# Rows of the expert stages sent through DRAM, norms of 24 tiles in the setup, x in one queue, the feed-forward bias on GpSimd

## The reference

```
x = x + 0.5 * ffn(norm(x))     # 512 hidden, weights binarized, exact gelu
x = x + gated_attention(norm(x))   # groups of 32, one head, relu squared + a linear part
x = x + 0.5 * ffn(norm(x))     # same weights
x = x + 0.5 * experts(norm(x)) # below
x = x + linear_attention(norm(x))  # 16 heads of 64
x = x + 0.5 * experts(norm(x)) # same weights
```

## Time and profile before

| | us |
|---|---|
| median of 3 runs (2285.88 to 2286.19) | 2286.04 |
| profiled execution | 2280.57 |
| its span | 2278.7 |
| setup, to the first transpose of ffn0 | 23.5 |
| ffn0, to the first transpose of gau1 | 109.7 |

### The profile page before, as it was taken

The page is one execution under the profiler, slowest core; times in us unless marked ns, Lnnn a source line. Parts: engine busy times, 40 slices in busy tenths (PEclk is TensorE's granted clock), DMA queues, the critical chain, the costliest instruction groups (busy, mean ns, idle before and its releaser), DMA issues. The chain is left out here.

```text
span 2278.7 us, 42519 instructions
## 1 busy us (share of the span) xinstructions
PE 2170.7 (95%) x13706; PEld 1748.3 (77%) x13706; DVE 1522.8 (67%) x4922; ACT 1242.7 (55%) x2504; POOL 690.7 (30%) x724
## 2 busy tenths in 40 slices
PE   5989998999999999899999999999999899999995
PEld 5978888977777777777777777877777777777775
DVE  6867776876777776556565566666666666777664
ACT  4645445754554554465566665666665444545542
POOL 0412222533575655500000000000100344665545
PEclk9999999999999999999999999999999999999998
DMA  8040000000111111200000000000000011111122
GB/s 276 0 176 0 0 0 1 2 10 22 36 41 43 37 38 44 56 7 0 0 0 0 0 0 1 1 1 1 1 1 1 12 28 40 46 51 49 51 55 73
DMA packets 70648, 68.44 MB, mean 30 GB/s; under 512 B 9312, under 2 KB 57952, under 8 KB 70112
## 3 DMA queue, kind: packets, MB, share of 16 engines
q1 hardware_dynamic: 60960, 47.62, 6.6%
q0 software_dynamic: 8192, 16.79, 3.2%
q10 hardware_dynamic: 1344, 2.16, 0.4%
HBM read 32.47 MB, written 34.08 MB: 29 GB/s over the span
## 5 line engine op out<-in xcount | busy, mean ns | idle before, releaser
L2034 ACT ACTIVATE moe_fc<-moe_bank,all_b_fc 128x380 f32<-128x380 f32 (+2 forms) x448 | 245.8, 549 | 277.7 <-PE moe_bank L1964 274.6
L2141 DVE SCALAR_TENSOR_TENSOR moe_act<-moe_bank,all_b_moe_gate,moe_fc 128x380 f32<-128x380 f32 (+2 forms) x448 | 256.7, 576 | 168.3 <-PE moe_bank L1968 101.4
L1980 PEld LDWEIGHTS moe_bank<-all_w_proj,moe_act 128*128 128x128 f32 x2560 | 300.0, 192 | 12.2 <-issue 2.4
L1980 PE MATMUL moe_bank<-all_w_proj,moe_act 128*128 128x128 f32 x2560 | 305.7, 276 | 2.0 <-DVE moe_expert_out L2150 2.0
L1803 POOL DMA_INDIRECT all_landed<-rows_out,all_take_at x256 | 271.7, 1061 | 117.9 <-issue 113.4
L1494 POOL COPY lin_xn_ones<-lin_xn 128x254 f32<-128x254 f32 x32 | 12.7, 398 | 720.7 <-PE lin_bank L1244 720.4
L2041 ACT ACTIVATE moe_act<-moe_act 128x760 f32<-128x760 f32 (+2 forms) x224 | 174.7, 780 | 93.2 <-DVE moe_act L2141 92.7
L1879 POOL TENSOR_SCALAR moe_hot<-all_slot_ids,moe_slot 128x608 fp32r<-128x608 f32 x112 | 203.3, 1824 | 68.3 <-DVE moe_slot L2118 33.7
L1388 ACT ACTIVATE lin_neg<-lin_bank 128x512 f32<-128x512 f32 x256 | 151.7, 592 | 105.5 <-PE lin_bank L1236 61.9
L1286 PEld LDWEIGHTS lin_bank<-lin_kv,lin_qT 128*128 128x128 f32 x1024 | 145.0, 192 | 74.4 <-issue 62.3
L1964 PE MATMUL moe_bank<-gau_rowsT,all_w_fc 128*128 128x380 f32 (+2 forms) x448 | 170.1, 461 | 1.6 <-ACTq L2045 1.6
(11 more groups left out here) (248 smaller groups left out, 4472.8 us busy)
## 6 DMA issues: line engine op xcount, KB each, us to landing
rows_out<-moe_expert_out SPq DMA_DIRECT2D x96, 128.0 KB
rows_out<-all_zeros SPq DMA_DIRECT2D x1, 9728.0 KB, 28.7
rows_out<-moe_expert_out SPq DMA_DIRECT2D x80, 62.0 KB
all_landed<-rows_out,all_take_at POOLq DMA_INDIRECT x256, 2.7
out<-all_x SPq DMA_DIRECT2D x5, 640.0 KB, 4.5
all_w_fc<-in_w_fc SPq DMA_DIRECT2D x1, 2048.0 KB, 9.8
all_w_gate<-in_w_gate SPq DMA_DIRECT2D x1, 2048.0 KB, 13.6
all_w_proj<-in_w_proj SPq DMA_DIRECT2D x1, 2048.0 KB, 18.1
```

What stands on the lines that cost most here:

```text
L1980: last = nc.tensor.matmul(bank[OUT][:, j * DIM:(j + 1) * DIM], act_in[:, i % 2, h, j * P:(j + 1) * P], k.w_proj[:, e * MC + h, :], start=( ...
L2034: nc.scalar.activation(fc[:, j, 0:c.width], bank[FC + j % 2][:, 0:c.width], ACT.Identity, bias=k.b_fc[:, e * MC + j:e * MC + j + 1]).then_ ...
L2141: nc.vector.scalar_tensor_tensor(act_in[:, i % 2, j, 0:c.width], bank[GATE + j % 2][:, 0:c.width], k.b_moe_gate[:, e * MC + j:e * MC + j + ...
```

## The change

1. **Rows through DRAM.** Four DRAM tensors `rows_in` (`RINGS`, 609 rows of 128) take turns. After `assign`, GpSimd issues for each tile and choice an indirect DMA that scatters the 128 rows of the norm to their places (4 per batch). SyncE waits for them, and loads both halves back in blocks of 128 rows (4 DMAs per batch; 304 rows are two blocks and a third that overlaps). `send` transposes those blocks, three per half. Split, one-hots and their semaphores go; SyncE follows the slots.
2. **Slots.** Batches are routed every 4 slots instead of 5 (8 instead of 9 in the last routing chunk); load stands at lag 8, the sends at 14 and 15. Gathers and combines stay where they are. Four norms are kept instead of three.
3. **Setup.** Parts of x are 12, 12, 20 and 20 tiles, all on SyncE's queue, and the setup makes the norms of 24 tiles. ffn0 takes the statistics of part 3 in turns 0 to 4 and of part 4 in turns 8 to 12, four tiles a turn, with the norm chain's pieces in turns 4 to 7 and 12 to 15.
4. **Bias on GpSimd in ffn0**, as in ffn2; the group bias is made two buckets a turn in turns 4 to 19, spread at turn 21, and the weight difference stands at turn 28. Its inputs have a semaphore of their own, first in SyncE's queue.
5. Stage gau1 fills the four rings with zeros behind `rows_out`; GpSimd and SyncE wait for that once.

```diff
-X_PART = 16
+X_CUTS = 0, 12, 24, 44, 64
 KNOWN = 2
 LANDED = 4
+RINGS = 4
...
-                for i in range(KNOWN):
-                    sp.dma_start(k.x[:, X_PART * i:X_PART * (i + 1), :], xv[:, X_PART * i:X_PART * (i + 1), :]).then_inc(k.x_in[i], 16)
+                for i in range(4):
+                    sp.dma_start(k.x[:, X_CUTS[i]:X_CUTS[i + 1], :], xv[:, X_CUTS[i]:X_CUTS[i + 1], :]).then_inc(k.x_in[i], 16)
...
-                for i in range(KNOWN, 4):
-                    act.dma_start(k.x[:, X_PART * i:X_PART * (i + 1), :], xv[:, X_PART * i:X_PART * (i + 1), :]).then_inc(k.x_in[i], 16)
...
-                k.norms[0].columns(dve, chain, 0, X_PART * KNOWN)
+                k.norms[0].columns(dve, chain, 0, X_CUTS[KNOWN])
...
+                if first:
+                    pool.wait_ge(late, 1)
+                for b in range(3):
+                    bias(b)
+                for b in range(BATCHES):
+                    if b + 3 < BATCHES:
+                        bias(b + 3)
+                    if route:
                         routing.on_gpsimd(pool, b)
+                    elif 4 <= b < 20:
+                        group_bias.add(pool, 2 * (b - 4), 2 * (b - 4) + 2)
+                    elif b == 21:
+                        pool.wait_ge(biased.sem, biased.at(b + 3))
+                        group_bias.spread(pool)
+                    elif b == BATCHES - 4:
+                        weights_less_last_row(k, pool, last_row, wv1_done)
...
-                    add_bias(b)
+                    stats(b)
...
-                        if b < 16:
-                            if b % 8 == 0:
-                                dve.wait_ge(k.x_in[KNOWN + b // 8], 16)
-                            for t in range(TILES):
-                                last = stats_of(k, 16 + b, t)
-                            if b % 8 == 7:
+                        part, step = KNOWN + b // 8, b % 8
+                        if part == 4:
+                            continue
+                        lo, hi = X_CUTS[part], X_CUTS[part + 1]
+                        if step < 5:
+                            if step == 0:
+                                dve.wait_ge(k.x_in[part], 16)
+                            for i in range(lo + 4 * step, lo + 4 * step + 4):
+                                last = nc.vector.bn_stats(k.stats[:, i, :], k.x[:, i, :])
+                            if step == 4:
                                 last.then_inc(late, 1)
                                 dve.wait_ge(late, 2 + b // 8)
-                        if b >= 8 and b % 8 < PIECES:
-                            norm.piece(dve, chain, 16 + 2 * b - 2 * (b % 8), 32 + 2 * b - 2 * (b % 8) if b < 16 else X_TILES, b % 8)
+                                norm.piece(dve, chain, lo, X_TILES if part == 3 else hi, 0)
+                        else:
+                            norm.piece(dve, chain, lo, X_TILES if part == 3 else hi, step - 4)
...
-FIRST_PLAN = Plan((4, 5, 5, 5, 5, 5, 3), (5, 5, 5, 5, 5, 9), (None, (11, 5), (11, 5), (11, 5), (11, 5), (11, 5), (16, 5)))
-LAST_PLAN = Plan((4, 5, 5, 5, 5, 5, 3), (5, 5, 5, 5, 5, 9), (None, (11, 5), (11, 5), (11, 5), (11, 5), (11, 5), (15, 4)))
+FIRST_PLAN = Plan((4, 5, 5, 5, 5, 5, 3), (4, 4, 4, 4, 4, 8), (None, (11, 5), (11, 5), (11, 5), (11, 5), (11, 5), (16, 5)))
+LAST_PLAN = Plan((4, 5, 5, 5, 5, 5, 3), (4, 4, 4, 4, 4, 8), (None, (11, 5), (11, 5), (11, 5), (11, 5), (11, 5), (15, 4)))
...
-ROUTE_LAGS = {"norm": 0, "transpose": 1, "router": 2, "mask": 3, "count": 4, "assign": 5, "hot0": 8, "hot1": 9,
-              "send0": 10, "send1": 11}
-SENDS = "send0", "send1"
+ROUTE_LAGS = {"norm": 0, "transpose": 1, "router": 2, "mask": 3, "count": 4, "assign": 5, "load": 8, "send0": 14, "send1": 15}
...
-                    later = how.route_step[c.n] == 5 and b != follow[-1]
                     for what, lag in ROUTE_LAGS.items():
-                        work[i * how.route_step[c.n] + lag + (later and what in SENDS)][what] = b
+                        work[i * how.route_step[c.n] + lag][what] = b
...
+                def load(b):
+
+                    sp.wait_ge(scattered[(b - OWN) % RINGS], scattered_at(b))
+                    if b - 2 >= OWN:
+                        sp.wait_ge(sent_ps, 2 * (b - 2) + 2)
+                    ring = k.rows_in[(b - OWN) % RINGS]
+                    for h in range(2):
+                        lo = 1 + h * HALF
+                        sp.dma_start(arrive[:, (b - OWN) % 2, h, 0:HALF_BLOCKS - 1, :],
+                                     ring[lo:lo + HALF_WHOLE, :].rearrange("(j p) d -> p j d", p=P)).then_inc(arrived[(b - OWN) % 2], 16)
+                        sp.dma_start(arrive[:, (b - OWN) % 2, h, HALF_BLOCKS - 1, :],
+                                     ring[lo + HALF - P:lo + HALF, :]).then_inc(arrived[(b - OWN) % 2], 16)
...
+                for c, slots in order:
+                    for s, work in slots:
+                        i = c.n * EXPERTS + s // MC
+                        if "load" in work:
+                            load(work["load"])
+                        if s % MC == MC - 1 and i:
+                            keep(i - 1)
+                            if out is not None and (i - 1) % EXPERTS == EXPERTS - 1 and 2 * EXPERTS - 1 <= i - 1:
+                                store(plan[(i - 1) // EXPERTS - 1])
+                keep(UNITS - 1)
...
+                def scatter(b):
+                    ring = (b - OWN) % RINGS
                     pool.wait_ge(xn_ready, b + 1)
                     pool.wait_ge(routed, b + 1)
+                    if b - RINGS >= OWN:
+                        pool.wait_ge(arrived[(b - OWN) % 2], arrived_at(b - RINGS))
+                    for t in range(TILES):
+                        for h in range(TOP_K):
+                            nc.gpsimd.indirect_dma_start(k.rows_in[ring], bass.IndirectOffsetOnAxis(slot[:, ring, t, h:h + 1], 0),
+                                                         xn[:, b % XN, t, :], None, bounds_check=EXPERTS * CAP,
+                                                         oob_is_err=False).then_inc(scattered[ring], 16)
...
-                        pe.wait_ge(split_done, b + 1)
+                        pe.wait_ge(arrived[(b - OWN) % 2], arrived_at(b))
                     pe.wait_ge(sent_sb, 2 * b + h)
-                    for t in range(TILES):
-                        if h == 0:
-                            pe.wait_ge(hot_sb, TILES * b + t + 1)
-                        for q in range(2):
-                            last = nc.tensor.matmul(bank[SENT][:, 0:HALF], parts[:, b % PARTS, q, t, :],
-                                                    hot[:, b % 2, t, h * HALF:(h + 1) * HALF],
-                                                    start=(t == 0 and q == 0), stop=(t == TILES - 1 and q == 1))
+                    for j in range(HALF_BLOCKS):
+                        at = min(j * P, HALF - P)
+                        last = nc.tensor.transpose(bank[SENT][:, at:at + P], arrive[:, (b - OWN) % 2, h, j, :], k.ident[:, :])
```

More of the change, by code:

```diff
@@ L1896, in _ @@
                     for s, work in slots:
[L1897 to L1898 removed]
                         if "assign" in work:
[L1900 removed]
+                            scatter(work["assign"])
                         if "gather" in work:
@@ L2177, in _ @@
                             assign(work["assign"])
-                        for t in range(TILES):
-                            if f"hot{t}" in work:
-                                second_choice(work[f"hot{t}"], t)
                         if "combine" in work:
@@ L2249, in program @@
         k.slot_ids = k.sb("slot_ids", [P, EXPERTS * CAP])
+        k.rows_in = [nc.dram_tensor(f"rows_in{r}", (EXPERTS * CAP + 1, DIM), F32, kind="Internal").ap() for r in range(RINGS)]
         k.zeroed = k.dma_sem("zeroed")
```

138 lines of the change are left out of this document (55 added, 83 removed).

## The result

| | before, us | after, us |
|---|---|---|
| median (lowest to highest) of 4 runs each | 2285.96 (2284.01 to 2286.19) | 2261.11 (2257.78 to 2265.89) |
| profiled execution | 2280.57 | 2262.34 |
| its span | 2278.7 | 2260.5 |
| expert stages, ScalarE's first to last up bias, moe3 and moe5 | 471.0 and 470.4 | 465.6 and 463.6 |

The ratio is 0.9899 (95% interval 0.9885 to 0.9914): 24.9 us faster, where the forecast was 34.4. The time lies inside the range and 9 us above the forecast, within the 2244 to 2262 that I had given to the likeliest case. A second set of four runs gave 2263.22, just outside those, and a ratio of 0.9905 (0.9890 to 0.9920).

What follows compares the result with a forecast made beforehand. TensorE, busy 95% of the span, was taken to bound the kernel; 34 + 5 - 12 + 4.9 + 2.5 = 34.4 us off the 2286.0 median gave 2252 us, likeliest 2244 to 2262, eight in ten 2236 to 2277.

Steps and rivals of the forecast that it cites:

- Sends (34): Expert stages: 112 sends become three transposes of 0.33 us instead of four matmuls, gaining 0.30 each, 34 us; bounds 8 and 35.
- relief (5): Expert stages: one-hots leave VectorE, a split and comparisons leave GpSimd, so norms come sooner: gain 5 us, between 0 and 9.
- GpSimd's new chain (12): Expert stages: scatters beside gathers make combines wait, 1.2 us lost in each of ten chunks: 12 us, between 0 and 27.
- New path of the rows (0): Expert stages: scatter to DRAM and loads back stay hidden, tightest at batch 4 with 1.1 us to spare: cost 0.
- Setup (4.9): Setup: one queue and 12-tile parts let VectorE end at 13.1 instead of 18.0: gain 4.9 us, bounds 1.3 and 5.
- feed-forward (2.5): First feed-forward stage: bias add moves to GpSimd, relieving VectorE; weight difference costs 1.4 at turn 28: gain 2.5, bounds 0 and 4.
- (a): Expert stages: no stall, down projections swallow the late combines and the 12 us come back: 2240 us; chance 0.16.
- (b): Expert stages: GpSimd groups of 5.5 us and scatters landing 2 us later cost 24 us more: 2276 us; chance 0.17.
- (c): Expert stages: a scatter's issue on GpSimd is dearer than a gather's; at 1.4 us each, 2326 us; chance 0.08.
- (d): Expert stages: combines lengthen GpSimd's issues beside them, 7 us a chunk, 70 more: 2322 us; chance 0.02.
- (e): Sends: a transpose costs a full weight load, so the gain is 8 us instead of 34: 2278 us; chance 0.07.
- Signs named: Wrong if scatter issues aren't 1.0 us, TensorE waits on loads, or slots 4 to 26 don't shrink from 50.3 to about 48.5.

Runs made afterwards that it cites:

- G: Changed kernel with a chunk's first three combines one slot later and the fourth two slots later: 2231.40 us, ratio 0.9766 to before.
- D: Changed kernel with combines a slot later, gathers a slot earlier and each send's three transposes made twice: 2269.77 us, ratio 0.9936.
- U: Changed kernel with the setup of before (parts of x of 16 tiles, two queues, norms of 32 tiles): 2266.87 us, ratio 0.9926.
- E: Changed kernel with the bias add of the first feed-forward stage back on VectorE: 2267.55 us, ratio 0.9930.
- kernel C: Changed kernel with the first four combines of a chunk one slot later and every gather one slot earlier: 2240.70 us, ratio 0.9807.
- kernel S: Changed kernel with ScalarE's second silu of a unit put behind the next unit's first bias: 2251.74 us, ratio 0.9856.

## Why the prediction was right in sign and its time 9 us too low

**How near it came.** In the expert stages the forecast was 34 + 5 - 12 = 27 us and the profiles show 12.2: a miss of 15. The medians show one of 9.5 only because they differ by 6.7 us more than the profiles do, and no row gives that to a part of the change. That the time lies within the likeliest band is so in part luck.

**Sends (34) and relief (5): right in sum.** Together 42.5 measured against 39 (of it 6.0 are waits of TensorE in chunks 1 to 5 of before, all gone in G). The 0.33 for three transposes stands in the timeline and in D. How the 42.5 divide between the two wasn't taken apart.

**GpSimd's new chain (12): the step that failed.** It was put at 12 us, bounds 0 and 27, and cost 30.3. Its first half was right nearly to the tenth. In chunk 2 of moe5, from the start of slot 4: first scatter at 5.5, last issue of the first gather group at 14.6 (forecast 14.4), combine at 17.4 (17.2), and 0.7 us lost at slot 13 (0.7). At the fourth gather: last issue at 51.3 (50.8), combine at 54.7 (53.6), product ready at 57.0 (56.0), needed at 55.8 (55.3). Here the sum said "again 0.7, but the same 0.7 if it was lost before", and a down projection was to hide the rest. Three things were wrong in that. The rows took 3.4 us from issue to VectorE, not 2.8, and the last issue came 0.5 later, so the product's wait was 1.25 here. The forecast followed VectorE and TensorE through the late combine but not ScalarE, whose silu waits for the same product and holds the next bias behind it: 0.7 more in a chunk, and a second stop close behind the first. And after the double stop the granted clock fell in three of the ten chunks, 1.4 us in chunk 1 of moe5 and about as much in the others. Slots 27 to 30 lost 2.2 us in chunk 2 of moe5 and 4.2 in chunk 1 (10.6 and 12.7 against G's 8.4 and 8.5), where the sum had nothing beyond the 0.7 of slot 13.

**New path of the rows (0): right.** TensorE never waited for `arrive`. The Trainium skill (DMA: Bandwidth & Descriptors, the breakdown of a DMA's fixed cost) calls HBM the heaviest target for the write receipt; by that alone a scatter would land later than a gather into SBUF. The rows show the reverse: scatters land 2.3 us after their issue, the gathers of before 2.8. A gather also reads its rows from DRAM, and no run takes the two sides apart.

**Setup (4.9) and feed-forward (2.5): right in sum, within the spread.** Up to the first transpose of gau1 they took 133.2 us before and 125.5 and 127.7 after: 7.7 and 5.5 gained for the 7.4. By U and E neither part alone is shown to bring its figure. First transpose at 18.42 (forecast 18.6), statistics over 24 tiles in one run of 4.73 from 8.74. The first 10 us carried 228 GB/s in the one queue; for the 150 of the lower bound there was no row. Stage ffn0 2.6 us shorter in the first profile, 1.3 in the second. The stop at turn 28 that I priced at 1.4 did not come: behind the weight difference TensorE stood 0.57, and it stands 0.52 at that place in the kernel before.

**Rivals.** (a), no stall: wrong for the change, right for G, which it priced within 9 us (2240 against 2231). (b), 2276: half of its mechanism, more lost per chunk, was there, by other causes; groups were 5.2 and scatters early. (c) fell: scatter issues of 0.97. (d) fell: 76 of the 480 scatter and gather issues overlap a combine, and the longest of them took 1.12; one at 1929.49 took 1.00 beside the combine of 1929.64. The Trainium skill (SBUF — State Buffer, who interferes with whom) has a VectorE instruction with two SBUF inputs contend with a GpSimd instruction that reads SBUF, not with one that only writes it, and infers that building a DMA's descriptors takes only the write side. The rows of the combines agree: no issue of 1 us is held up by their four instructions of 0.35. The one-hots of the kernel before don't fit so well, with two SBUF inputs as well: of its 116 gather issues that overlap one, 25 took over 1.2 us, the longest 1.6. (e) fell by D.

**Signs named.** Slot 4 to slot 26 shrank from 50.3 to 48.0 (1912.25 to 1960.23), forecast 48.5. TensorE's loss was to be 1 us a chunk; it was 3. None of the three signs that I had named for being wrong came: they look at the scatter's issue, the loads and the way up to slot 26, and the loss lay behind it.

## What to carry to other kernels

When a wait is put into an in-order engine, follow everyone who waits for what is queued behind it, to the end: here the late product held not only TensorE but the silu on ScalarE, and with it a bias that had nothing to do with it. A stop that seems hidden to within a microsecond isn't priced by its own length only: two stops close together cost the clock as well in three of ten chunks. And a reader who waits belongs behind the work that others need: two lines that moved four combines of a chunk by one or two slots were worth more (32 us) than the change itself (25).

## What was not expected of the hardware

The granted clock fell to its lower level behind stops of TensorE of 1.78, 1.35 and 1.30 us, each with one of 0.43 behind it (0.61 over the 4 us shown above), in the second profile behind 1.86 and 2.23 with the same 0.43, and behind a single one of 2.2 (kernel C). It stayed at 1.00 behind 1.08 and 0.43, but also behind 1.43 and 0.43, and behind a single 1.83 (kernel S). So the length of a stop alone doesn't decide it; what else does isn't shown. A scatter of 128 rows of 512 bytes to DRAM is issued in 0.97 us and lands in 2.3, both a little less than a gather's 1.0 and 2.8. From ScalarE's last up bias of moe3 to its first of moe5, nearly all of it the linear attention stage, which the change leaves alone, pass 829.4 us in the profile of before and 830.0 to 833.7 in those of the other kernels: up to 4 us of any comparison of two profiles need not be the change's.
